# Emitting the next phase's LayerNorm subtiles behind the output projection instead of ahead of the FFN chain

## What is computed

```python
xn    = layernorm(x)
# attention part: a scan over time, one state vector of 16 per channel
delta = softplus(xn @ Wd.T + bd)
a_pos = softplus(a_log) + 1e-4
state = exp(-delta * a_pos) * state + delta * b_param * xn   # per token
y     = state.sum(-1)
attn  = y @ Wo.T + bo
# FFN part
real  = xn @ cos(theta + theta_noise)
imag  = xn @ sin(phi + phi_noise)
out   = x + attn + sqrt(real**2 + imag**2)
```

## Time and profile before

| what | value |
|---|---|
| runs of the kernel before | 1107.92 and 1104.95 us, median 1106.43 |
| the profiled execution | 1103.29 us |
| its span, slowest core (core 3) | 1101.5 us |
| spans of the cores | 1089.2 to 1101.5 us |
| mean granted TensorE clock of the cores | 0.707 to 0.726 |
| DVE busy | 817.2 us (74%) |
| PE busy | 582.1 us (53%) |
| ACT busy | 582.2 us (53%) |
| POOL busy | 150.9 us (14%) |

### The profile page before, as it was taken

How to read it: one execution, slowest core, us unless ns; L and a number is a source line. 1 busy time by engine, 2 the same in 40 slices (tenths; PEclk the granted TensorE clock), 3 DMA queues, 4 the chain that set the end, 5 groups by cost and what they waited for, 6 DMA issues and landing times.

```text
span 1101.5 us, 9304 instructions; the slowest of 8 cores (1089.2 to 1101.5 us)
## 1 busy us (share of the span) xinstructions
PE 582.1 (53%) x2248; PEld 245.1 (22%) x2248; DVE 817.2 (74%) x721; ACT 582.2 (53%) x924; POOL 150.9 (14%) x127
## 2 busy tenths in 40 slices
PE   1323343445467554565555447656655555454785
PEld 1211011112123231222122114433221221121343
DVE  4279888989842449999999992434799999999423
ACT  5785766776633235656665543323456555565330
POOL 2468000000012100000000001211000000000232
PEclk9855556556678766766775568977767766666799
DMA  8877100000012310000000002231100000000023
GB/s 237 211 226 218 35 26 29 29 20 1 0 48 87 95 36 0 1 1 0 1 0 1 0 0 70 83 115 53 34 0 1 0 1 0 1 0 1 29 72 115
DMA packets 36324, 51.66 MB, mean 47 GB/s; under 512 B 3120, under 2 KB 19760, under 8 KB 36272
## 3 DMA queue, kind: packets, MB, share of 16 engines
q1 hardware_dynamic: 33584, 42.68, 13.3%
q0 software_dynamic: 2688, 8.39, 2.2%
HBM read 42.67 MB, written 8.39 MB: 46 GB/s over the span
## 4 chain that ended last, share of the span: by engine, by line
DVE 42%; PE 19%; issue 18%; ACT 17%; DMA 2%; DVEq 1%; POOL 0%; ACTq 0%; SPq 0%; POOLq 0%
DVE grot L838 34%; ACT abar L787 10%; PE pd L961 6%; PE pt L649 3%; PE pt L659 3%; DVE sfm L975 2%; DMA xsub<-xin 2%; ACT bdg_bf L177 2%; PE py L989 1%; PE pe L377 1%; PE pd L296 1%; DVE xsub L439 1%; PE pt L377 1%; PE py L377 1%; ACT L822 1%
## 5 line engine op out<-in xcount | busy, mean ns | idle before, releaser
L838 DVE TENSOR_TENSOR_SCAN grot<-abar,gcar,vbuf 128x768 bf16<-128x768 f32 (+1 forms) x380 | 652.0, 1776 | 41.7 <-ACT abar L787 33.8
L787 ACT ACTIVATE abar<-delta,nega 128x768 f32<-128x768 f32 (+1 forms) x380 | 336.7, 896 | 239.8 <-DVE grot L838 238.2
L876 PE MATMUL pe<-grot,bdg_bf 128*128 128x384 bf16 x256 | 84.6, 429 | 116.6 <-DVE grot L838 116.5
L876 PE MATMUL py<-grot,bdg_bf 128*128 128x384 bf16 x256 | 82.3, 421 | 113.0 <-DVE grot L838 112.9
L296 PE MATMUL pd<-xnbf,wd_bf 128*128 128x384 bf16 (+1 forms) x368 | 99.2, 451 | 21.4 <-ACT xsub L315 15.5
L961 PE MATMUL pd<-ybf,wo_bf 128*128 128x384 bf16 (+1 forms) x320 | 75.2, 387 | 0.0
L863 PE MATMUL py<-grot,bdg_bf 128*128 128x512 bf16 x64 | 33.6, 539 | 75.7 <-DVE grot L838 75.7
L863 PE MATMUL pe<-grot,bdg_bf 128*128 128x512 bf16 x64 | 34.3, 543 | 71.1 <-DVE grot L838 71.1
L723 POOL TENSOR_TENSOR xsub<-r,i 128x384 f32<-128x384 f32 (+1 forms) x9 | 18.1, 2010 | 383.0 <-ACT i L715 383.0
L296 PEld LDWEIGHTS pd<-xnbf,wd_bf 128*128 128x128 bf16 x368 | 49.7, 136 | 71.3 <-issue 64.6
L876 PEld LDWEIGHTS pe<-grot,bdg_bf 128*128 128x128 bf16 x256 | 18.6, 102 | 177.3 <-issue 174.8
(11 more groups left out here) (114 smaller groups left out, 645.7 us busy)
## 6 DMA issues: line engine op xcount, KB each, us to landing
xsub<-xin SPq DMA_DIRECT2D x14, 512.0 KB, 4.4
xres<-xin SPq DMA_DIRECT2D x32, 192.0 KB, 2.4
out<-osub POOLq DMA_DIRECT2D x32, 192.0 KB, 2.6
xres<-xin SPq DMA_DIRECT2D x8, 256.0 KB, 3.5
out<-osub POOLq DMA_DIRECT2D x8, 256.0 KB, 3.1
etmp<-tht SPq DMA_DIRECT2D x6, 256.0 KB, 4.9
r<-thn SPq DMA_DIRECT2D x6, 256.0 KB, 5.7
r<-pht SPq DMA_DIRECT2D x6, 256.0 KB, 4.7
```

The costliest lines, as they stand in the source:

```text
L787: sx = run("scalar", lambda e, sl=sl_ab, par=par, dt=dt, n=n, tp=tp: e.activation(out=abar[:, sl * TP:sl * TP + tp], in_=delta[:, par * TP ...
L838: vs = run("vector", lambda e, g=gsl, sl=sl_ab, par=par, dt=dt, n=n, tp=tp: e.tensor_tensor_scan(out=grot[:, g * TP:g * TP + tp], data0=ab ...
L876: td = run("tensor", lambda e, c=c, g=gsl, dt=dt, n=n, bb=ypair[c]: e.matmul(bb[:, 0:384], bdg_bf[:, (dt * NST + n) * P:(dt * NST + n + 1) ...
```

## The change

The block that emits the subtiles moves from right behind `emit_ffn_mm` to behind the eight matmuls of the output projection, ahead of `sfm`. So on every engine's list:

- TensorE: the 8 matmuls of the projection now come before the 8 transposes of a subtile.
- ScalarE: the four instructions of `emit_ffn_chain` now come before Ln, Exp and the two bf16 copies of a subtile.
- SyncE: the load of `xres` now comes before the load of `xsub`.
- VectorE and GpSimd: the order stays as it is.

What is computed, the buffers and the schedule `a_sched` stay the same.

```diff
@@ -930,13 +930,6 @@
                 dt, c0, wdth = cjobs[it]
                 if NFC + it < nch:
                     emit_ffn_mm(NFC + it)
-                if p + 1 < NPH:
-                    for ts_ in a_sched.get(it, []):
-                        if ts_ not in a_done_set[p + 1]:
-                            ev_xnbf_free_t = ffn_ti[0]
-                            emit_a_subtile(p + 1, ts_,
-                                           [pe[1], py[1]], [("pe", 1), ("py", 1)])
-                            a_done_set[p + 1].add(ts_)
                 b = it % 2
                 tok0 = PSTART[p] + c0
                 xrs = it % 2
@@ -964,6 +957,13 @@
                         ybf[:, k * TP + c0:k * TP + c0 + w],
                         start=(k == 0), stop=(k == NDT - 1)),
                         "T" if k == NDT - 1 else None)
+                if p + 1 < NPH:
+                    for ts_ in a_sched.get(it, []):
+                        if ts_ not in a_done_set[p + 1]:
+                            ev_xnbf_free_t = ffn_ti[0]
+                            emit_a_subtile(p + 1, ts_,
+                                           [pe[1], py[1]], [("pe", 1), ("py", 1)])
+                            a_done_set[p + 1].add(ts_)
                 slot = it % 2
                 jr = rslot(it)
                 wait("vector", "T", tw)
```

## The result

The changed kernel takes 1107.7 us (median of 36 runs) against 1104.4 for the kernel before (35 runs beside them). The ratio is 1.0034, 95% interval 1.0023 to 1.0044: 3.7 us slower (0.34% of 1104.4), within 2%. The ratios use only executions in which neither die of four cores lagged behind the other. The prediction said 1112, +5.6 us on a median of two runs that was itself 2.0 us above the later one of 35.

The account below looks back on a forecast made before the run. It took the tail loops as paced by chains of short handovers, no engine full, with `sfm` stalled by the projection. Terms -19.1 + 8.9 + 0.6 + 15.5 = +5.9 us on the 1106.4 median gave 1112 us; range 1098 to 1120.

Parts of the forecast that it names:

- the two costs: Tail loops: ScalarE's queue delays subtiles, +8.9 us; matmuls and transposes restarting at TensorE's slow clock, +15.5 us.
- Part 1: Ten subtile iterations of both tails: projection ahead of the transposes removes VectorE's idle time before `sfm`, -19.1 us.
- Part 2: Five subtile iterations with an FFN chain: subtile's Ln on ScalarE waits behind the chain's Exp, +8.9 us.
- Line 429 right behind line 732: Sign on ScalarE: subtile's first instruction, the Ln, directly follows the FFN chain in five iterations.
- the restart: FFN matmuls after each of five subtile iterations start at the slow clock, 1.8 us each, +9.0 together.
- Part 3: SyncE's queue: subtile load behind `xres` arrives late in it 9 of the second tail, +0.6 us.
- Part 4: TensorE in the tails: after waits, FFN matmuls and transposes run at the slow clock, +15.5 us.
- The end of the second tail: Projection of it 12 and the delta matmuls behind it start slow, between 1.3 and 2.6, taken as +2.0 us.
- clock holds: Rival: in the tails the projection is hidden and the clock costs nothing, -9.6 us, 1097 us; chance 0.22.
- ScalarE costs nothing: Rival: subtile's Ln starts as early as today and the clock holds, -18.5, 1088 us; chance 0.03.
- nothing moves: Rival: `sfm` also waits for something else ending with the projection, so the reorder is idle, 1106 us; chance 0.09.
- Whole next iteration slow: Rival: all FFN matmuls behind a subtile iteration run at the slow clock, +20, 1126 us; chance 0.11.

Follow-up runs that it names:

- e5_after_fill: Changed kernel plus unused matmuls between projection and subtile's transposes (14 in iterations with a chain, 10 before other subtiles); 1094.1 us, ratio 0.9893 against the kernel before.

## Why the prediction came out as it did

**The direction and the two costs were right, the sum was too large by 1.9 us.** It was +5.6 us with the chances on "within 2%"; measured is +3.7, and the interval excludes both no change and the forecast sum. As a time, 1112 lies 7.6 us above the median of before that was measured beside the changed kernel, about twice what was found. The step that failed is the sum: terms read on one core, the slowest, of one execution were added up as if they were the metric's, and put on a median of two runs. The term mis-sized most is part 1.

**Part 1 (-19.1 us): right in mechanism, wrong in size.** `sfm` follows the copy without idle time in all ten iterations. But -19.1 is core 3's idle time, the most of the eight: over the cores it is 14.7 to 19.1 and 16.8 in the mean. What made up for it is a gain that the prediction had put at nothing. In the five steps without a chain the sum had -10.1 of idle time and gave back some 0.7 for slow `sfm` transposes and 0.6 for a load, so -8.8; the eight-core mean is -10.8, although the mean idle time there was only 9.3. The copies of line 387 also wait 1.6 us less in these five steps for the subtile's own transposes: with the projection run ahead, the wait before the transposes is shorter and they are in part still at the full clock, in it 9 of the second tail as follows, against 1.08 and 1.06 us behind 4.38 before. The addition of line 1001 waits 0.9 us more behind slow `sfm` transposes.

```profile
742.34 0.63 PE L377 MATMUL pe<-csts,xsub 128*128 128x128 f32 x4 [3.08 <-DVE xsub L439]
742.80 0.91 PE L377 MATMUL py<-csts,xsub 128*128 128x128 f32 x4
```

**Part 2 (+8.9 us): right, shown alone.** ScalarE's reorder by itself costs 8.1 us. "Line 429 right behind line 732" holds in four of the five iterations on the slowest core; in it 3 of the second tail the load was later than the chain (VectorE waited 3.76 us for it), so the chain was hidden. But the size of it 4, 3.15, was only the delay at the full clock. In the eight-core mean its step grew by 6.5 us with ScalarE's list alone: 3.1 us of delay at the full clock, the rest from matmuls and transposes that ran at the slow clock. In the changed kernel it grew by 4.9 (the sum had -0.45 + 3.15 there, with 1.8 + 0.35 for the restart: 4.85).

**Part 3 (+0.6 us): wrong, it is nothing.** In it 9 (slowest core) bn_stats follows `osub` with no wait for `xsub`, although the load was issued one iteration later (734.00, used at 738.68), and with SyncE's order of before the time is the same within the intervals.

**Part 4 (+15.5 us): right for the two moves together, not for TensorE's alone.** The four steps behind a subtile without one of their own grew by 1.8, 2.3, 2.3 and 2.6 us; the sum had 1.8 and 0.35 each, 2.15. The end of the second tail was +2.0 and is +2.8, less 0.4 later. The filled waits show the cause: with them 14 instead of 40 cosine groups are slow, and the kernel is 15.5 us shorter. What the prediction did not see is that this price hangs on part 2. By its terms TensorE's reorder alone is parts 1 and 4, -19.1 + 15.5 = -3.6 us; measured is -13.3, and -10.6 in the mean of the cores' spans. There the steps behind a subtile grew by 5.3 us, not 8.9, and step 4 of the second tail by 0.5. The rule from the Trainium skill, TensorE: Matmul & The Clock Gate, section "HAM oscillation — how this bites in real kernels", is that bursts shorter than the waits between them start slow each time. The trace agrees for the cosine groups behind the waits, 40 of 40 slow in the changed kernel, 0.50 in it 2; it does not for the transposes of it 1 of the second tail, fast (0.63 and 0.60 us) directly behind 3.66 us of waiting. The rival "clock holds" (1097) would have needed what e5_after_fill had to buy with 130 more matmuls; it took 1094.

**What failed is the step from terms to the metric.** By groups of steps in the eight-core mean, the forecast against the measurement: the five steps without a chain -8.8 and -10.8; steps 1, 3, 1 and 3 -1.4 and -0.6; step 4 of the second tail 4.85 and 4.9; the four behind subtiles 8.6 and 8.9; the rest 2.7 and 2.4. That is +5.9 against +4.8, so errors of up to 2 us cancelled in part, which is luck.

The time is that of the slowest core. Over 21 runs of the kernel before, the slowest core lies 4.7 us above the mean of the eight (1102.4 against 1097.7); over 37 of the changed kernel 3.6 (1106.2 against 1102.6), over 11 on the same chip as the 21 3.3. The mean core lost 4.9 us, and the slowest 3.8. A likely reason, not shown by an experiment: a slow core is one whose waits met the slow clock more often (core 3 had 19.1 us of idle time before `sfm`, core 1, the fastest, 14.7), and had more to win from their removal. With ScalarE's list alone it is 12.3 in the mean against 8.1. So the two lists alone add up to -5.2 us in the metric and to +1.7 in the mean of the cores (-10.6 and +12.3), where both together measure +3.7 and +4.9: 3.2 us are the moves' effect on each other, the rest lies in the spread of the cores. Second, the sum was added to a median of two runs, 2.0 us above that of 35. The miss of 4.3 us in the time itself (1112.0 against 1107.7) is these 2.0, the 1.1 of the cores' spread, and about 1 in the terms.

The rivals: "ScalarE costs nothing" and "nothing moves" are excluded by the experiments with one list each. "Whole next iteration slow" (1126) did not come: the projection of the iteration behind took 1.46 to 1.59 us with 384 columns.

## What to carry to other kernels

A call that emits work for five queues is five moves: moved as a whole, this one put a gain of 13 us (TensorE's list) and a loss of 8 (ScalarE's list) together and came out 4 slower, not 5 faster. In part this is because the second move lengthens the waits behind which the first one pays. Each list could be moved by itself. Put work that somebody waits for ahead of work that is read iterations later, above all on an in-order engine with a wait inside (here for GpSimd). And when work is hidden in front of a wait of TensorE's, look at what runs first behind the wait: it inherits the slow clock that the moved work used to pay for.

## What was not expected of the hardware

Matmuls whose result is thrown away made the kernel faster: by 8 us with TensorE's list alone (ratio 0.988 to 0.9805), by 15.5 in the changed kernel (1.0034 to 0.9893). In e5_after_fill a wait filled down to 0.64 us kept the granted clock at 1.00 over the following transposes and a further gap of 1.63 us (it 1 and 2, core 4); the same 0.64 us did so on six of eight cores, and on two the next eight matmuls took 2.60 and 2.76 us. What decides between them no run here shows. And the spread between the cores of one execution is itself a part of the metric: with the same program on each, the spans went from 1089.2 to 1101.5 us in the profiled execution before, and only from 1108.5 to 1111.8 in that of ScalarE's list alone.
